# A graph network in one kernel: at most two scatters on their way, and four sets of blocks in place of three

## The chip, the cores and the metric

The kernel runs on one core of one Trainium2 chip. The metric is the device time of one execution in microseconds (us): 5878.37 us before the change, the median of 3 runs (5878.09 to 5882.56). Engine names are those of the profile: PE (matmul) and PEld (its weight load), DVE (vector), ACT (scalar), POOL (GpSimd), SP (the engine that issues most DMAs).

## The reference, cut to what matters

A graph has 6250 nodes with 128 features and 106,250 edges, sorted by destination. Four residual blocks follow each other, each on `h = relu(layernorm(x))`:

```
deg[i]  = number (or summed weight) of the edges into i;  dinv = rsqrt(deg)
gcn(h, W, b): (segment_sum of (h@W)[src] * dinv[src]*dinv[dst] over dst) + b
x += L0: gcn whose edge weights are sigmoid(gelu([h_src,h_dst]@w1+b1)@w2+b2)
x += L1: relu(gcn(relu(gcn(h, W1, b1)), W2, b2))
x += L2: m = relu(h@Wm1+bm1)@Wm2+bm2; agg = segment_sum(m[src]); MLP of [h, agg]
x += L3: gcn(relu(gcn(relu(gcn(h)))))
```

After L0 there are six sums over the same edges. They all use the same matrix of edge counts, and so the kernel builds this matrix once.

## The kernel before, in words

Nodes stand in 49 blocks of 128 (`DB = 49`). The work has these stages, each in program order on its engine.

**Preparation** (about 90 us): lists of sources and destinations, layernorm of the nodes, a table in DRAM.

**First pass over the edges** (220 groups of 4 tiles of 128 edges). POOL gathers rows of the table with indirect DMAs (`gather`, L655), PE and ACT and DVE make the edge weights, and PE sums the degrees. Beside it DVE and ACT find repeated edges inside runs of 1024 edges (`compare`, `dedupe`), which leaves for each edge a count (`count16`) and an address in the count matrix `adj` (`place`). SP stores rows for the second pass, and zeroes `adj`, one block per four groups.

**Scatters.** When POOL has issued its last gather it runs `scatter(g)` for g = 0 to 207 (L663 to L669): four indirect DMAs each, one per column `s`, 832 in all. Each writes 128 counts of two bytes to `adj` in DRAM. Before scatter k POOL waits until scatter k-4 has landed (`after(pool, scattered[s], 16 * g)`, L667, one semaphore per column), and for `s = 0` also for `deduped`. The waits stand in POOL's own stream, and nothing but scatters is behind them.

**Second pass over the edges** (220 groups again). PE spreads dinv of the sources (L963), DVE picks (`pick`, L1399), ACT weighs one-hot matrices (`weigh`, L771), PE sums rows (`sum_rows`, L972), DVE adds them (L1413). Then the L0 result is finished (`conv`), all in about 110 us.

**Dense stage.** The six sums are q = 0 to 5. For each block of destinations w, PE multiplies the 49 chunks of `adj` (as `halves` in SBUF, loaded by SP, five buffers of up to 25 chunks, `AR = 5`) with the node features, kept as three bf16 parts: one matmul of 128x128 by 384 columns per chunk (L1030). The list `UNITS` (L71 to L79) sets the order for all engines:

- *whole*: all 49 chunks of block w of sum q, then one matmul that adds the rows of `spare` (L1040), then DVE reduces the three parts (`reduce_sum`, L1499) and makes the next layer's input.
- *spare*: edges that cross runs have their counts in an extra block. There is one extra block for each set of destination blocks (`SETS`), because a set may begin before the scatters of the next set have landed. A spare unit of q = 0 takes 49 matmuls, a split on DVE, and a sum of the counts into `spare_sum` (`combine`, L1520), which q > 0 uses.
- *early*: part of the chunks of a block of sum q = 1, done between the sets of q = 0. DVE reduces them and adds them to `acc` (`take_early`, L1532 to L1536). The *late* unit of q = 1 does the rest.

In q = 1 (the message layer) each block is normalized before it goes on: DVE runs `take_sums` (reduce, two scalar_tensor_tensor, L1490 to L1496 with a square root on ACT between), PE turns the result (`turn_source`, L1053) after two thirds of the *next* unit's chunks, then multiplies (`up`, L1064); `down` (L1073) follows after the first third of the unit after. After its own `take_sums` DVE does `set_table` of the block before (L1571, L1503 to L1506). PE's order is written out in the loop at L1085 to L1106, which cuts each unit's chunks in three parts (`cuts`).

Before it loads the spare block of a set, SP reads from `needed` how many scatters must have landed and waits for them (L583 to L591).

Of the kernel before, what the change touches and what calls it, by code (L numbers as in the profile page):

```python
# [44 lines left out]

DB = -(-N // P)

SETS = ((0, 26), (26, 41), (41, 49))
EARLIER = len(SETS) - 1
SPARE = DB  # L50
BLOCKS = DB + len(SETS)
ROW_BITS, SRC_BITS = 13, 6
# [14 lines left out]

EARLY = [[(0, 24, 0, 25)], [], []]  # L70
UNITS = []  # L71
for n, (w0, w1) in enumerate(SETS):
    UNITS += [(0, SPARE + n, 0, DB, "spare")] + [(0, w, 0, DB, "whole") for w in range(w0, w1)]
    UNITS += [(1, w, c0, c1, "early") for b0, b1, c0, c1 in EARLY[n] for w in range(b0, b1)]

LATE_C = {w: max((c1 for one in EARLY for b0, b1, c0, c1 in one if b0 <= w < b1), default=0) for w in range(DB)}
for q in range(1, LAYERS):
# [15 lines left out]
def after(eng, sem, value):  # L93

    if value > 0:
        eng.wait_ge(sem, value)
# [10 lines left out]
def build(nc, a, out):  # L107
# [13 lines left out]
    with ExitStack() as ctx, ExitStack() as early:  # L121
# [3 lines left out]
        def sem(name):  # L125
            return ctx.enter_context(nc.semaphore(name))
# [273 lines left out]
        scattered = [sem(f"scattered{s}") for s in range(S)]  # L400
# [210 lines left out]
        def _(pool):  # L611
# [51 lines left out]
            def scatter(g):  # L663
                pool.wait_ge(deduped, g // RUN_TILES + 1)
                for s in range(S):
                    k = g * S + s
                    after(pool, scattered[s], 16 * g)  # L667
                    nc.gpsimd.indirect_dma_start(out=adj[:, :], out_offset=bass.IndirectOffsetOnAxis(ap=place[:, k:k + 1], axis=0),  # L668
                                                 in_=count16[:, k:k + 1], in_offset=None).then_inc(scattered[s], 16)  # L669

# [5 lines left out]
            for g in range(SCATTERS):  # L676
                scatter(g)
# [173 lines left out]
        def _(pe):  # L851
# [154 lines left out]
            def add_sources(u, c0, c1):  # L1006
                q, w, u0, u1, kind = UNITS[u]
                for c in range(c0, c1):
                    if c == u0:
                        after(pe, reduced, u - 2)  # L1010
                    if q > 0 and kind == "spare":
                        if c == 0:
                            pe.wait_ge(combined, 2 * len(SETS))
                        if c == DB - 2:
# [96 lines left out]
        def _(dve):  # L1111
            made = [0]

            def link(instruction):

                made[0] += 1
                instruction.then_inc(prep, 1)
                dve.wait_ge(prep, made[0])
# [19 lines left out]
            for n in range(EARLIER):  # L1138
                last = nc.vector.tensor_scalar(in_sets[:, n, :], last_window[:, :], float(SETS[n][1]), None, ALU.is_lt)
            link(last)  # L1140
# [101 lines left out]
            nc.vector.tensor_tensor(in_runs, of_runs, ps_carry_b.unsqueeze(2).to_broadcast([P, SLOTS, RUN_TILES]), ALU.is_equal)  # L1242
            link(nc.vector.tensor_scalar(late[:, :], ps_carry_b, float(P * SETS[0][1]), None, ALU.is_ge))
            for n in range(1, EARLIER):
# [376 lines left out]
```

## Time and profile before

| | us |
|---|---|
| median of 3 runs | 5878.37 |
| profiled execution, its time | 5869.91 |
| its span on the core | 5868.2 |
| PE busy / DVE busy / ACT busy / POOL busy | 3758.9 / 2498.4 / 1229.7 / 1736.7 |
| matmul L1030, 14553 of them | 2476.2 busy |
| scatters L668, 832 of them | 869.1 busy, 270.5 idle ahead of them |

The span is cut into 40 slices of 146.7 us. The page shows PE busy to 3 or 4 tenths in slices 1 to 10, near 0 in slices 11 to 18, and to 9 tenths from slice 22 to the end; POOL is busy to 7 tenths in slices 8 to 17 and then stops. Since matmuls overlap, two figures are kept apart: the mean length of one (326 ns) and the distance from one to the next.

### The profile page before, as it was taken

The page shows a single profiled execution, that of the slowest core. Times are in us where ns is not written, and L with a number is a line of the kernel's source. Part 1 is how long each engine was busy: PE and PEld are TensorE (multiplying, and loading weights), DVE is VectorE, ACT ScalarE, POOL GpSimd, SP SyncE. Part 2 cuts the span into 40 slices and gives each one's busy share as a digit, 9 for nine tenths or more (in the row PEclk, how much of TensorE's full clock was granted, in tenths as well). Part 3 has the DMA queues.
Part 4 walks back from the last instruction along what each step waited for, and adds up shares of the span by engine and source line. Part 5 has one row for each costly group of instructions (what it writes and reads, how often), then busy time and mean ns, then how long its engine had stood idle before and what let it go on. Part 6 is the DMA issues. An engine that isn't in the chain of part 4 may idle for free.

```text
span 5868.2 us, 82106 instructions
## 1 busy us (share of the span) xinstructions
PE 3758.9 (64%) x26427; PEld 2570.5 (44%) x26427; DVE 2498.4 (43%) x11277; ACT 1229.7 (21%) x3130; POOL 1736.7 (30%) x1749
## 2 busy tenths in 40 slices
PE   3444444444000000007667999999999999999999
PEld 2333333333000000006555666666666666666666
DVE  6666766676101000009997222454344333333111
ACT  2454444444000000005554000111111000000000
POOL 4665666666777777760000000000000000000000
PEclk7555555555555555559998999999999999999999
DMA  5777777776100000007772565455555566566665
GB/s 151 233 228 232 230 232 224 232 231 207 22 1 23 11 7 11 11 8 231 238 236 98 177 193 181 160 164 176 160 165 167 170 191 192 181 190 191 187 199 170
DMA packets 456936, 925.35 MB, mean 158 GB/s; under 512 B 81052, under 2 KB 318060, under 8 KB 449868
## 3 DMA queue, kind: packets, MB, share of 16 engines
q1 hardware_dynamic: 382668, 830.57, 44.1%
q0 software_dynamic: 69312, 87.75, 6.2%
q8 instruction: 230, 3.77, 0.3%
q10 hardware_dynamic: 4544, 1.77, 0.1%
q14 instruction: 182, 1.49, 0.1%
HBM read 739.99 MB, written 179.87 MB: 157 GB/s over the span
## 4 chain that ended last, share of the span: by engine, by line
PE 46%; another core or an unknown queue 24%; DVE 16%; issue 8%; ACT 3%; DVEq 1%; DMA 0%; SPq 0%; ACTq 0%
PE ps L1030 40%; DVE same L1296 3%; DVE inv_all L1399 3%; PE ps L1064 1%; ACT apart L746 1%; DVE onehot_b L1327 1%; DVEq L478 1%; PE ps L1073 1%; DVE scaled L1339 1%; DVE acc L1413 1%; DVE h L1413 1%; ACT apart L749 1%; PE ps L1040 1%; DVE pre L1335 1%
## 5 line engine op out<-in xcount | busy, mean ns | idle before, releaser
L1030 PE MATMUL ps<-parts,halves 128*128 128x384 bf16 x14553 | 2476.2, 326 | 6.1 <-DVE parts L1470 5.6
L1030 PEld LDWEIGHTS ps<-parts,halves 128*128 128x128 f16 x14553 | 1425.4, 98 | 887.8 <-DVE parts L1470 7.1
L660 POOL DMA_INDIRECT rows<-table,src_of x880 | 842.7, 958 | 583.9 <-DVE pre L1335 299.9
L668 POOL DMA_INDIRECT adj<-count,place x832 | 869.1, 1045 | 270.5 <-issue 270.5
L1499 DVE TENSOR_REDUCE summed_f<-ps 128x128 f32<-128x384 f32 x277 | 154.5, 558 | 1394.8 <-PE ps L1040 1307.7
L940 PE MATMUL ps<-dst_mlp,onehot_t 128*128 x2640 | 364.5, 232 | 562.0 <-issue 329.5
L963 PE MATMUL ps<-inv_parts,low_t 128*128 128x49 bf16 x2640 | 130.7, 189 | 673.3 <-issue 523.9
L940 PEld LDWEIGHTS ps<-dst_mlp,onehot_t 128*128 128x128 bf16 x2640 | 275.8, 104 | 640.7 <-issue 583.9
L1399 DVE SCALAR_TENSOR_TENSOR inv_all<-chunk_iota,chunk_of,ps 128x49 f32<-128x49 f32 x880 | 181.9, 263 | 798.9 <-remote 796.8
L771 ACT ACTIVATE onehot<-plain,norm 128x128 f32<-128x128 bf16 x880 | 281.0, 390 | 1016.5 <-issue 754.3
L1296 DVE SCALAR_TENSOR_TENSOR same<-spare_sum,key,ps 128x128 bf16<-128x128 f32 (+2 forms) x832 | 488.1, 588 | 6.5 <-DMA spare_sum<-key_list 6.3
L972 PE MATMUL ps<-rows,onehot 128*128 128x128 f32 x1760 | 286.0, 298 | 267.2 <-issue 264.8
L954 PE MATMUL ps<-weight_parts,onehot_b 128*128 128x4 bf16 x880 | 132.5, 185 | 483.1 <-DVE weight_parts L1362 243.3
L963 PEld LDWEIGHTS ps<-inv_parts,low_t 128*128 128x128 bf16 x2640 | 94.2, 98 | 726.5 <-issue 540.1
L825 ACT COPY source_t<-ps 128x128 f32<-128x128 f32 x196 | 52.2, 266 | 1610.1 <-PE ps L1053 1610.1
L972 PEld LDWEIGHTS ps<-rows,onehot 128*128 128x128 f32 x1760 | 241.3, 205 | 276.0 <-issue 273.1
L954 PEld LDWEIGHTS ps<-weight_parts,onehot_b 128*128 128x128 bf16 x880 | 92.0, 105 | 562.6 <-issue 540.3
L720 ACT COPY onehot_t<-ps 128x512 bf16<-128x512 bf16 x220 | 128.2, 583 | 907.6 <-remote 732.1
L1335 DVE TENSOR_TENSOR pre<-ps,rows 128x256 f32<-128x256 f32 x220 | 91.8, 417 | 284.9 <-remote 284.9
L746 ACT ACTIVATE apart<-spare_sum,key 128x768 bf16<-128x768 f32 x208 | 204.2, 982 | 13.8 <-DMA spare_sum<-key_list 4.8
L749 ACT ACTIVATE apart<-apart,ones 128x768 bf16<-128x768 bf16 x208 | 205.6, 988 | 6.8
L1327 DVE TENSOR_SCALAR onehot_b<-window_iota_b,local_dst 128x128 bf16<-128x128 bf16 x880 | 162.8, 259 | 0.0
(255 smaller groups left out, 3586.7 us busy)
## 6 DMA issues: line engine op xcount, KB each, us to landing
halves<-adj SPq DMA_DIRECT2D x297, 800.0 KB, 4.5
halves<-adj SPq DMA_DIRECT2D x297, 768.0 KB, 4.4
adj<-slot_of SPq DMA_DIRECT2D x52, 1568.0 KB
h_rows<-rows SPq DMA_DIRECT2D x220, 256.0 KB
rows<-h_rows SPq DMA_DIRECT2D x220, 256.0 KB
spare_sum<-key_list SPq DMA_DIRECT2D x104, 512.0 KB
onehot_list<-onehot_b SPq DMA_DIRECT2D x220, 128.0 KB
low_row<-low_list SPq DMA_DIRECT2D x220, 128.0 KB
```

The source lines that it names most:

```text
L660: nc.gpsimd.indirect_dma_start(out=rows_0[:, g % RING, s, :], out_offset=None, in_=table[:, :], in_offset=bass.IndirectOffsetOnAxis(ap=src ...
L668: nc.gpsimd.indirect_dma_start(out=adj[:, :], out_offset=bass.IndirectOffsetOnAxis(ap=place[:, k:k + 1], axis=0), in_=count16[:, k:k + 1], ...
L746: nc.scalar.activation(apart[:, 0:r, :], key_row[:, n % KEYS, 0:r, :], ACT.Abs, bias=key[:, t:t + 1], scale=-1.0).then_inc(distant, 1)
L749: nc.scalar.activation(apart[:, 0:r, :], apart[:, 0:r, :], ACT.Relu, bias=ones[:, 0:1], scale=-1.0, accum_out=cross[:, batch % 2, r * S + ...
L771: last = nc.scalar.activation(onehot[:, g % SUMS, s, :], plain[:, g % KEPT, s, :], ACT.Copy, scale=norm[:, g % NORMS, s:s + 1])
L940: last = nc.tensor.matmul(ps_mlp[:, g % 2, s, :], onehot_t[:, g % 2, s, :], dst_mlp[:, bass.ds(window[s], 1), part, :].rearrange("p o m -> ...
L954: last = nc.tensor.matmul(ps_deg[:, bass.ds(window[s] * (PARTS + 1), PARTS + 1)], onehot_b[:, g % HELD, s, :], weight_parts[:, g % 2, s, : ...
L963: last = nc.tensor.matmul(ps_inv[:, g % 2, s, :], low_t[:, g % 2, s, :], inv_parts[:, part, :], start=part == 0, stop=part == PARTS - 1)
L972: last = nc.tensor.matmul(products[:, g % SUMS, s, :], onehot[:, g % SUMS, s, :], rows[:, g % RING, s, :], start=True, stop=True)
L1030: last = nc.tensor.matmul(ps_sum[u % 3], halves[:, n % AR, c - at, :], parts[q % 2][:, c, :, :].rearrange("p t d -> p (t d)"), start=(c == ...
L1296: nc.vector.scalar_tensor_tensor(same[r % 2][:, 0:r + 1 - r0, :], key_row[:, n % KEYS, r0:r + 1, :], key[:, t:t + 1], ps_weight[:, CROSS - ...
L1399: last = nc.vector.scalar_tensor_tensor(inv_all[:, s, :], chunk_iota[:, 0, :], chunk_of[:, k:k + 1], ps_inv[:, j, s, :], ALU.is_equal, ALU ...
```

## The change

Two things. POOL waits, ahead of scatter k, also for scatter k-2 to have landed (`s - 2` is -2 or -1 for the first two columns, which names columns 2 and 3 of the group before). And `SETS` has four sets in place of three, with other early units: 26 blocks of 25 chunks after the first set, 10 of 25 and 36 of 10 after the second, 9 of 35 (in two loads) after the third.

```
-SETS = ((0, 26), (26, 41), (41, 49))
+SETS = ((0, 26), (26, 36), (36, 45), (45, 49))
-EARLY = [[(0, 24, 0, 25)], [], []]
+EARLY = [[(0, 26, 0, 25)], [(26, 36, 0, 25), (0, 36, 25, 35)], [(36, 45, 0, 35)], []]
 (in scatter(g), for each s:)
                     after(pool, scattered[s], 16 * g)
+                    after(pool, scattered[s - 2], 16 * (g + 1 if s >= 2 else g))
                     nc.gpsimd.indirect_dma_start(out=adj[:, :], ...)
```

An entry of `EARLY` is (first block, end of blocks, first chunk, end of chunks). `LATE_C` (L76) takes from it where the late unit of a block begins: chunk 25 for blocks 0 to 23 before; chunk 35 for blocks 0 to 44 after. `BLOCKS`, the number of blocks of `adj` that are zeroed, goes from 52 to 53, and `EARLIER` from 2 to 3.

## Rows read from the trace of the kernel before

**Rows 1.** Busy time by stage: us, PE, PEld, DVE, ACT, POOL, PEclk, DMA share, GB/s.
```profile
1475.00:1811.00 336.00, 15.14 (x109) 11.01 (x109) 33.78 (x123) 16.07 (x32) 256.51 (x254) 0.50 0.05 9
1811.00:2615.00 804.00, 72.80 (x322) 49.27 (x322) 30.45 (x200) 19.16 (x60) 612.55 (x579) 0.50 0.05 11
2615.00:3085.00 470.00, 298.48 (x3962) 261.38 (x3962) 427.82 (x2782) 253.03 (x793) 0.00 (x0) 0.95 0.72 222
...
3196.00:5868.00 2672.00, 2665.62 (x17018) 1721.44 (x17016) 887.16 (x2937) 205.68 (x735) 0.00 (x0) 1.00 0.57 179
```

**Rows 2.** Waits between 1475 and 2615 us: total, times, longest.
```profile
ACT onehot L771 <- issue: 754.3, 15, 54.7
DVE inv_all L1399 <- remote: 732.5, 15, 54.7
```

**Rows 3.** Groups of POOL: all scatters.
```profile
L668 POOL DMA_INDIRECT adj<-count,place x832 | 869.1, 1045 | 270.5 <-issue 270.5
```

**Rows 4.** Timeline within the scatters: start, length, instruction, idle before.
```profile
2131.04 0.98 POOL L668 DMA_INDIRECT adj<-count,place  x1 [0.30 <-issue]
2132.32 0.97 POOL L668 DMA_INDIRECT adj<-count,place  x1 [0.31 <-issue]
```

**Rows 5.** Timeline of PE and PEld a little later.
```profile
2142.66 0.10 PEld L963 LDWEIGHTS ps<-inv_parts,low_t 128*128 128x128 bf16 x1 [2.69 <-issue]
2144.06 0.20 PE L963 MATMUL ps<-inv_parts,low_t 128*128 128x49 bf16 x1 [2.60 <-issue]
```

**Rows 6.** The last scatter, in the timeline of POOL.
```profile
2613.34 1.09 POOL L668 DMA_INDIRECT adj<-count,place  x1 [0.30 <-issue]
```

**Rows 7.** DMA busy tenths from 2613 to 2617 us, 0.1 us per digit.
```profile
DMA  0000001100000000000011000000000000000000
```

**Rows 8.** The first gather of the first pass, in the timeline.
```profile
90.11 1.25 POOL L660 DMA_INDIRECT rows<-table,src_of  x1 [41.84 <-DMA table<-acc]
```

**Rows 9.** DMA busy tenths from 87 to 91 us, 0.1 us per digit.
```profile
DMA  9988998300000000028300000000000000000000
```

**Rows 10.** Another restart of POOL, in the timeline.
```profile
30.66 1.16 POOL L652 DMA_INDIRECT acc<-src_list,tile_of  x1 [18.36 <-DMA dst_list<-lists]
```

**Rows 11.** GB/s of the DMAs from 27 to 31 us, 0.1 us per figure.
```profile
GB/s 323 333 312 225 215 220 195 189 190 149 133 128 128 128 118 108 102 92 77 67 61 51 26 20 5 0 0 0 0 0 0 0 0 0 0 0 0 0 0 0
```

**Rows 12.** A gather released by a compute engine, in the timeline.
```profile
1451.12 0.42 DVE L1335 TENSOR_TENSOR pre<-ps,rows 128x256 f32<-128x256 f32 x1
...
1451.81 0.95 POOL L660 DMA_INDIRECT rows<-table,src_of  x1 [3.22 <-DVE pre L1335]
```

**Rows 13.** Two early units of 25 chunks, in the timeline of DVE.
```profile
3440.57 0.56 DVE L1499 TENSOR_REDUCE summed_f<-ps 128x128 f32<-128x384 f32 x1 [3.12 <-PE ps L1030]
...
3444.63 0.56 DVE L1499 TENSOR_REDUCE summed_f<-ps 128x128 f32<-128x384 f32 x1 [3.12 <-PE ps L1030]
```

**Rows 14.** One late unit of 24 chunks, in the timeline of all engines.
```profile
3842.47 0.56 DVE L1499 TENSOR_REDUCE summed_f<-ps 128x128 f32<-128x384 f32 x1 [1.02 <-PE ps L1040]
...
3845.41 0.14 PEld L1053 LDWEIGHTS ps<-ident,source 128*128 128x128 f32 x1 [0.32 <-issue]
3845.44 0.30 PE L1053 MATMUL ps<-ident,source 128*128 128x128 f32 x1
...
3846.38 0.29 DVE L1506 TENSOR_TENSOR parts<-left_d,parts 128x128 bf16<-128x128 f32 x1
...
3846.88 0.61 PE L1064 MATMUL ps<-source_t,w_L_gnn_Wm 128*128 128x128 f32 x4
...
3847.69 0.56 DVE L1499 TENSOR_REDUCE summed_f<-ps 128x128 f32<-128x384 f32 x1 [1.01 <-PE ps L1040]
```

**Rows 15.** Two whole units of q = 1, in the timeline of DVE.
```profile
3893.29 0.56 DVE L1499 TENSOR_REDUCE summed_f<-ps 128x128 f32<-128x384 f32 x1 [4.45 <-PE ps L1040]
3902.41 0.56 DVE L1499 TENSOR_REDUCE summed_f<-ps 128x128 f32<-128x384 f32 x1 [4.45 <-PE ps L1040]
```

**Rows 16.** The third spare unit of q = 0, in the timeline of PE.
```profile
3678.37 8.13 PE L1030 MATMUL ps<-parts,halves 128*128 128x384 bf16 x49
```

## The prediction

> **What bounds the kernel now.** I read first the busy time by stage [rows 1]. It shows three regimes. From 3196 us to the end PE is busy for 2665.6 of 2672 us: the dense stage is bound by PE alone, at full clock. From 2615 to 3085 us the second pass over the edges runs, bound by DVE (428 of 470 us). From 1475 to 2615 us POOL does the scatters, and nothing else makes headway: PE 88 us, DVE 64 us of 1140. Then the waits of that stretch [rows 2]: fifteen waits of up to 54.7 us on ACT and on DVE, 754 and 733 us in total; those on DVE are put down to something outside the engines. Fifteen groups of the second pass get done there, at 56 us each (the longest wait and one round of work), where later each takes 470/205 = 2.3 us. The timeline shows how: PE brings an instruction to its start every 1.4 us, a weight load at 2142.66 and its matmul at 2144.06 [rows 5], while POOL starts a scatter every 1.28 us and idles 0.30 us between two [rows 4]. A group of the second pass needs 40 PE instructions (20 matmuls, 20 loads), and 40 x 1.4 = 56 us. It ends when the scatters do. So the path is: first pass, all 832 scatters, second pass, dense stage. Every us on the scatters is a us on the kernel, and so is every us for which PE waits in the dense stage; the DMAs are not full in either (0.05 and 0.57).
>
> One thing follows at once. The dense stage begins at 3196 us, 580 us after the last scatter [rows 6]. Sets exist so that the dense stage may begin before all scatters have landed; no such wait is there to be shortened, and the new sets and early sums can only cost.
>
> **Part 1, the second wait.** It adds no transfer. First, does it hold anything back? The last scatter starts at 2613.34 [rows 6], and its packets move from 2615.0 to 2615.2 [rows 7]: 1.86 us from its start to the end of its data. The scatter before it started 1.40 us earlier, and its packets lie at 2613.6 to 2613.8, as far behind its own start. At 1.28 us a scatter [rows 4], scatter k-2 began 2.56 us before k does and has had its data written 0.7 us before. So two at a time is what is on the way already. The wait costs only what it takes POOL to go on from it. Today the wait is for k-4, whose data ended 3.2 us ahead, and POOL's stream can have instructions ready while it works; with the new wait the next scatter can't be made ready before k-2 has landed, which is when k-1 is nearly done.
>
> What a restart takes, from both sides. Low: a gather released by DVE starts at 1451.81, when DVE ended at 1451.54 [rows 12]: 0.27 us. Then k could start 1.86 + 0.27 = 2.13 us after k-2 (some tenths more for the semaphore of a DMA), less than 2.56, and the wait is free. High: two restarts from a landing. The data that the first gather waited for ended at 89.0 [rows 9], and it started at 90.11 [rows 8]: 1.11 us. In the other, the data ended at 29.5 [rows 11] and the indirect DMA started at 30.66 [rows 10]: 1.16 us. With 1.16, two scatters take 1.86 + 1.16 = 3.02 us, 1.51 each. Now one takes (869.1 + 270.5)/832 = 1.37 us [rows 3], so the high end is 832 x 0.14 = +117 us; a few scatters that DVE's work holds back add some, and I keep +130. By the row of 1.11 it is 2.97/2 = 1.485 and 832 x 0.115 = +96. A gain from the wait alone would need PE to be let go; that is the first rival. This is the same kind of instruction waiting for a DMA, so I go by these rows and not by that of 0.27; but both were first of their kind after a long rest, and ran 1.25 and 1.16 us in place of 0.95, so I take off a fifth. **+75 us**. Behind POOL's wait stand only more scatters; who waits for them is PE, which is slow until they end. In 75 us more of this, 75/56 = 1.3 groups more get done, worth 2.3 us each: **-3 us**.
>
> The Trainium skill, "DMA: Bandwidth & Descriptors", section "Anatomy of one DMA — SWDGE (gpsimd) path", gives about 2.0 us of fixed cost to one DMA from POOL, most of it the receipt of the write, and 0.05 us to the dispatch. By these figures the new wait is met 0.5 us ahead of need and costs nothing: an estimate of +0 in place of +75. The first figure agrees with the 1.86 us of [rows 6, 7]; the second is far under the 1.1 us that [rows 8, 9] leave between data and start, of which it may be only a part.
>
> **Part 2, the fourth set.** One more spare unit of q = 0: 49 matmuls at 8.13/50 = 0.1625 us [rows 16] = **+8 us** on PE. Its split and the sum of the spare counts go on DVE beside the next unit's 49 matmuls, as they do now. One more block to be zeroed lies in the first pass, before the last gathers; DMAs are 0.72 busy there, and POOL does not wait for it. A fourth wait of SP for scatters is met 580 us before.
>
> **Part 3, early and late units.** The chunks are the same in number, so PE's matmuls are. Early: 26 x 25 + 10 x 25 + 36 x 10 + 9 x 35 = 1575 chunks against 600; late: 45 blocks of 14 chunks against 24 of 24. Early units follow each other on PE without a gap: 4.06 us for 25 chunks [rows 13], 0.1625 each. One of 10 chunks takes 1.63 us; DVE needs 0.56 + 0.35 us and two hops, about 1.0, so it still keeps up; SP loads 320 KB for each, with four loads ahead (6.5 us), where 800 KB land in 4.5 us on the page. So early units cost 0, and +10 if a load of small pieces falls behind (for the range).
>
> Late units are another matter. A whole unit of q = 1 takes 9.12 us [rows 15], so one of 24 chunks should take 9.12 - 25 x 0.1625 = 5.06; it takes 3847.69 - 3842.47 = 5.22 [rows 14]. The rest is PE waiting 0.3 us for DVE's chain (`take_sums`), which must be through before PE may turn the block: the turn starts 2.97 us behind the reduction. From there to the next reduction it is 2.25 us, of which 8 chunks are 1.30. With 14 chunks only 4 are left behind the turn: the period is 2.97 + 2.25 - 4 x 0.1625 = 4.57 us. Since the turn now waits for DVE's chain and the other 10 chunks are long done, nothing shortens it. DVE's own work per unit ends 3846.67 - 3842.47 = 4.20 us behind its start, less than 4.57, so it isn't the bound. PE alone would need 9.12 - 35 x 0.1625 = 3.43. It waits 1.14 us in each of 45 late units, 51 us, and no longer 0.16 in 24, 4 us: **+47 us**. Bounds: +35 if the two chains overlap better, +60 if PE's second step (L1064), which needs ACT's copy of the turned block, comes 0.2 late as well.
>
> **Sum.** 5869.9 + 75 - 3 + 8 + 47 = 5997 us for an execution like the profiled one. The runs' median lies 8 us above that execution; I forecast **6004 us** for the median. Less than 0.2% (12 us) can't be told from no change.
>
> **Rivals.**
> 1. *PE is let go: faster.* The pace of PE hangs on POOL's unbroken work: 1.4 us an instruction in the scatters, none of this after them. If gaps of 0.4 to 0.5 us between scatters in place of 0.30 let PE through, the second pass moves under the scatters. Wholly: the end of the first pass no longer takes 336 us [rows 1], the second pass (220 x 2.3 = 506) is over at about 2000 us, the dense stage starts at 2115 and ends at 2115 + 2672 + 55 = 4842, plus the waits of sets for scatters: about 4860. In part: at twice the pace the tail halves and the remaining 1047 us hold 37 groups, 22 more, 50 us: 5954, still slower. It decides from 127/2.3 = 55 groups more on, a pace of under 0.4 us. For it: the sets would then be of use, and the starving is tied to POOL. Against it: even gaps of 0.3 us at 1.4 us spacing free nothing now, one scatter is still always on its way, and two are already the most that are.
> 2. *The wait is free* (restart of 0.27 us): 6004 - 72 = 5932. This is also the case in which the wait does not do what it says, since no third scatter was ever on its way.
> 3. *The restart is dearer*, past 1.3 us, or two semaphores per instruction slow POOL: 1.6 us a scatter, +190: 6120.
> 4. *The late units don't wait*, because the trace's 0.3 us is no true bound: 6004 - 47 = 5957.
>
> **Chances.** My forecast 0.48 (its own range 5970 to 6055), rival 2 0.20, rival 4 0.07, rival 3 0.07, rival 1 0.14 of which three quarters end faster than before, 0.04 for things I don't see, spread over both sides. Faster by over 0.2%: 0.13; within 0.2%: 0.03; slower 0.84. Range 5910 to 6080: it holds the forecast, rivals 2 and 4 and the bounds of the late units, and leaves out most of rivals 1 and 3.
>
> **What the profile after would show.** Part 1: POOL idle per scatter 0.4 to 0.5 us in place of 0.3, scatters from 1475 to about 2690, and 56 us a group in the second pass as before. Part 2: four spare units of q = 0. Part 3: reductions 4.57 us apart in late units, 0.7 us or more of idle ahead of each turn, no idle of PE in early units. I am wrong if PE's instructions come closer than 1.4 us while POOL scatters, if scatters keep 1.37 us, or if late units take 3.4 us.

## The result, and the profile after

The changed kernel takes 5241.04 us, the median of 4 runs (5238.31 to 5247.42), against 5878.23 us for the kernel before in the same series. The ratio is 0.8918, with a 95% interval of 0.8907 to 0.8929: 637 us faster, where 126 us slower was forecast. The profiled execution took 5239.61 us with a span of 5237.9 us.

The page of the kernel after, busy tenths in 40 slices of 131 us:

```profile
PE   3444444444446666008987779899999999999999
POOL 3565665656653335664454541000000000000000
```

PE is no longer dark while POOL scatters: the second pass (slices 13 to 16) and the dense stage run beside scatters that go on as far as slice 25. Only two slices of PE are dark, 17 and 18. The groups of the scatters and of the dense matmuls, busy time and mean, and idle ahead of them with its releaser:

```profile
L670 POOL DMA_INDIRECT adj<-count,place x832 | 820.1, 986 | 874.1 <-DMA adj<-count,place 610.9 <-issue 263.2
L1032 PE MATMUL ps<-parts,halves 128*128 128x384 bf16 x14602 | 2490.0, 327 | 387.9 <-DMA halves<-adj 387.9
```

POOL now idles 874.1 us ahead of scatters in place of 270.5 [rows 3], and PE waits 387.9 us for `adj`, where the forecast had no such wait. Busy time by stage (columns as in [rows 1]):

```profile
1485.00:1521.00 36.00, 14.71 (x107) 10.70 (x106) 25.32 (x119) 16.38 (x34) 21.66 (x23) 0.50 0.20 59
1530.00:2030.00 500.00, 340.73 (x4376) 300.82 (x4376) 475.12 (x3070) 280.94 (x880) 193.25 (x199) 0.94 0.77 230
...
2115.00:2374.00 259.00, 0.00 (x0) 0.00 (x0) 8.76 (x51) 0.00 (x0) 169.07 (x175) 0.50 0.03 5
```

The end of the first pass, 109 matmuls that took 336 us [rows 1], is over 36 us after the first scatter (two of them fall a little later). The whole second pass then takes 500 us, 2.3 us a group, where fifteen groups took 56 us each [rows 2]. Meanwhile POOL starts 199 scatters in 500 us, one in 2.5 us, not in 1.37. So PE has nothing to do from 2102 to 2374: the dense stage waits for the scatters of its first set, and again ahead of the second and third set. These three waits are 384.2 of the 387.9 us. In the timeline of PE:

```profile
2374.17 4.14 PE L1032 MATMUL ps<-parts,halves 128*128 128x384 bf16 x15 [272.58 <-DMA halves<-adj]
...
2779.07 3.36 PE L1032 MATMUL ps<-parts,halves 128*128 128x384 bf16 x10 [52.42 <-DMA halves<-adj]
...
3038.94 6.33 PE L1032 MATMUL ps<-parts,halves 128*128 128x384 bf16 x26 [59.23 <-DMA halves<-adj]
```

**Where the time went.** In the kernel before the first scatter started at 1475 and the first dense matmul here:

```profile
3173.57 6.66 PE L1030 MATMUL ps<-parts,halves 128*128 128x384 bf16 x40
```

From first scatter (1475 and 1486) to first dense matmul it was 1698 us and is now 888: -810. The gathers end 11 us later (+11). From there to the last matmul of the dense loop it was 2688 us (3173.6 to 5861.9) and is now 2857 (2374.2 to 5231.5): +169, of which the waits of the later sets are 112, one more spare unit 8, and early and late units together 47: 45 late units at 4.56 us for what was 24 at 5.21 and 21 at 9.12, and 975 more chunks of 0.1625 us in early units. The sum is -630, which is what the two profiled executions differ by.

Two timelines of POOL show the scatters beside the second pass, and at its end, when nothing else moves data:

```profile
1645.75 0.97 POOL L670 DMA_INDIRECT adj<-count,place  x1 [2.53 <-DMA adj<-count,place]
1647.02 0.97 POOL L670 DMA_INDIRECT adj<-count,place  x1 [0.30 <-issue]
1650.87 0.97 POOL L670 DMA_INDIRECT adj<-count,place  x1 [2.88 <-DMA adj<-count,place]
...
2102.84 0.96 POOL L670 DMA_INDIRECT adj<-count,place  x1 [0.30 <-issue]
2104.44 0.97 POOL L670 DMA_INDIRECT adj<-count,place  x1 [0.64 <-issue]
2105.72 0.97 POOL L670 DMA_INDIRECT adj<-count,place  x1 [0.30 <-issue]
```

In quiet the gaps are 0.30 and 0.64 in turn, 2.88 us for two scatters, 1.44 each. Beside the second pass (DMA share 0.77) many gaps are 2.5 to 2.9 us: scatters land late among the loads of `rows` and `plain`, and POOL now stands until they have. By the semaphore events of the trace a scatter lands 2.13 us behind its start in quiet (2115 to 2374 us, median) and 4.0 us behind it beside the second pass (1530 to 2030 us).

### The profile page after: what moved, and what is told of

It reads as the page before. It is cut to its first block, busy times and chain, and to the rows that moved or that the text cites. A ratio compares the mean times of both kernels' runs of the same rounds, so it can differ in the third digit from the quotient of the medians.

```text
span 5237.9 us, 83120 instructions
## 1 busy us (share of the span) xinstructions
PE 3742.2 (71%) x26476; PEld 2553.8 (49%) x26476; DVE 2559.0 (49%) x11400; ACT 1230.5 (23%) x3130; POOL 1685.5 (32%) x1749
## 4 chain that ended last, share of the span: by engine, by line
PE 37%; POOL 20%; issue 20%; DMA 19%; DVE 3%; SPq 0%; POOLq 0%; ACT 0%; another core or an unknown queue 0%; DVEq 0%
PE ps L1032 32%; DMA adj<-count,place 19%; POOL rows L660 15%; POOL adj L670 5%; PE ps L1066 1%; PE ps L1042 1%; PE ps L1018 1%; PE ps L1078 1%; PE ps L1055 1%; PE ps L1075 1%; DVE summed_f L1501 0%; DVE norm_d L1553 0%; DVE source L1498 0%; DVE stats_d L1492 0%; DVE x L1554 0%
## 5 line engine op out<-in xcount | busy, mean ns | idle before, releaser
L1032 PE MATMUL ps<-parts,halves 128*128 128x384 bf16 x14602 | 2490.0, 327 | 387.9 <-DMA halves<-adj 387.9
L670 POOL DMA_INDIRECT adj<-count,place x832 | 820.1, 986 | 874.1 <-DMA adj<-count,place 610.9
L1501 DVE TENSOR_REDUCE summed_f<-ps 128x128 f32<-128x384 f32 x335 | 186.9, 558 | 1785.2 <-PE ps L1042 1195.2
L974 PE MATMUL ps<-rows,onehot 128*128 128x128 f32 x1760 | 269.0, 299 | 4.4 <-ACT onehot L773 4.4
L974 PEld LDWEIGHTS ps<-rows,onehot 128*128 128x128 f32 x1760 | 230.7, 205 | 5.0 <-ACT onehot L773 5.0
L965 PE MATMUL ps<-inv_parts,low_t 128*128 128x49 bf16 x2640 | 110.4, 189 | 165.5 <-DVE low_t L1393 103.0
L1345 DVE TENSOR_REDUCE logit<-scaled 128x4 f32<-128x256 f32 x220 | 92.4, 420 | 113.7 <-remote 69.0
```

Of the source, the lines that this page charges most:

```text
L965: last = nc.tensor.matmul(ps_inv[:, g % 2, s, :], low_t[:, g % 2, s, :], inv_parts[:, part, :], start=part == 0, stop=part == PARTS - 1)
L974: last = nc.tensor.matmul(products[:, g % SUMS, s, :], onehot[:, g % SUMS, s, :], rows[:, g % RING, s, :], start=True, stop=True)
L1032: last = nc.tensor.matmul(ps_sum[u % 3], halves[:, n % AR, c - at, :], parts[q % 2][:, c, :, :].rearrange("p t d -> p (t d)"), start=(c == ...
L1501: nc.vector.tensor_reduce(into, ps_sum[u % 3].rearrange("p (t d) -> p d t", t=PARTS), AX.X, ALU.add).then_inc(reduced, 1)
```

## The experiments

**A second level of the kernel before.** Each set of kernels below ran as one job on one chip, the kernel before among them. That kernel has two levels, and one job shows only one of them:

| job, chip | kernel before, us | kernels, us (ratio, 95% interval) |
|---|---|---|
| the result above | 5878.2 | after 5241.0 (0.892) |
| 1, chip 10 | 4555.7 | e1 5043.1 (1.107, 1.105 to 1.109); e2 4582.4 (1.006, 1.004 to 1.008); e3 4580.0 (1.005, 1.004 to 1.007); e4 4901.9 (1.076, 1.074 to 1.078) |
| 2, chip 8 | 5913.8 | e5 5912.8; e6 5280.9 (0.893, 0.891 to 0.894) |
| 3, chip 12 | 4557.1 | e7 5039.6 (1.107); e8 4581.9 (1.005); e9 4898.5 (1.076); e10 4664.6 (1.024, 1.022 to 1.026) |
| 4, chip 2 | 4555.9 | e11 4669.5 (1.024); e12 4583.3 (1.006) |
| 5, 6, 7, chips 15, 3, 1 | 4554.0, 4560.3, 4560.3 | e13 4924.0; e14 4936.6; e15 4938.4 |
| 8, chip 6 | 5879.9 | e16 5282.7 |
| 9, chip 3 | 5907.0 | e17 5900.3 |
| 10, chip 9 | 5875.0 | e18 5235.7 (0.891, 0.889 to 0.894) |

Call the level of 4556 us open and that of 5875 to 5914 us starved. Chip 3 was open in job 6 and starved in job 9, so the level does not belong to a chip. The kernels e5 and e13 to e17 ran once each.

**e1, e2: the wait alone, the sets alone.** e1 is the kernel before with the new wait; e2 is the changed kernel without it.

```
 e1   SETS, EARLY as before
+                    after(pool, scattered[s - 2], 16 * (g + 1 if s >= 2 else g))
 e2   SETS, EARLY as after
-                    after(pool, scattered[s - 2], 16 * (g + 1 if s >= 2 else g))
```

> The kernel before with the second wait alone; its three sets and 24 early units stay. Theory A (the wait lets PE go, the sets only make use of it): the second pass is over near 2110 us, as with the whole change; PE then waits for the scatters of blocks 0 to 25, as far as about 2380; after 27 units and 24 early ones (2380 + 220 + 98 = 2700) the next set needs 41/49 of the scatters, 700 of 832, near 2860 to 2900, 16 units take it to about 3010, the last set waits to about 3150 (the last scatter landed), and what is left of the dense stage is 2672 - 350 - 98 = 2224 us: 5300 to 5400 us. Rival B (the new sets and their early units are what lets PE go, or both are needed): PE is starved as before, and the time is 5878 plus the price of the wait, 5930 to 5960.

> The change without the second wait: four sets and the deeper early sums alone. Theory A: PE is starved as before, 56 us per group of the second pass until the last scatter near 2615; the time is that of before plus one spare unit (+8) and the late units (+47): 5878 + 55 = 5933, within 10. Rival B (the sets let PE go): 5240 or less.

Neither figure was met, since the job was open: the kernel before took 4556. The second pass of e2 there, by stage and in the timelines of POOL and PE:

```profile
1231.00:1725.00 494.00, 326.02 (x4361) 285.86 (x4362) 472.93 (x3052) 279.89 (x877) 348.37 (x360) 0.98 0.83 232
```
```profile
1399.13 0.96 POOL L668 DMA_INDIRECT adj<-count,place  x1 [0.30 <-issue]
1399.77 0.94 PE L972 MATMUL ps<-rows,onehot 128*128 128x128 f32 x7
1400.40 0.97 POOL L668 DMA_INDIRECT adj<-count,place  x1 [0.30 <-issue]
1401.52 0.48 PE L963 MATMUL ps<-inv_parts,low_t 128*128 128x49 bf16 x12 [0.80 <-DVE low_t L1391]
```

POOL starts scatters at 1.27 us with gaps of 0.30, as in [rows 4], and PE does 12 matmuls in 0.48 us beside them. So the cadence of POOL does not starve PE by itself; it does so in some jobs. In this job, where PE is free without it, the wait only costs. Beside the second pass e1 starts 193 scatters in 493 us, e2 360 in 494; PE waits three times for `adj`, 551.8 us in sum, and the kernel takes 487 us more. The sets and early sums cost 27 us there, half of the 55 put; the kernel before has no profile in an open job, so what they give back there is not known.

**e3, e8, e12: the second wait present but always met.** **e4, e9: one wait, for k-2. e10, e11: one wait, for k-3.**

```
 e3   after(pool, scattered[s], 16 * g)
      after(pool, scattered[s - 2], 16 * (g if s >= 2 else g - 1))
 e4   after(pool, scattered[s - 2], 16 * (g + 1 if s >= 2 else g))      and no other
 e10  after(pool, scattered[s - 3], 16 * (g + 1 if s >= 3 else g))      and no other
```

> The changed kernel with its second wait moved back by four scatters: scatter k waits for k-4 and for k-6. The instruction for the second wait is still in POOL's stream, but it never holds POOL back. Theory A (what counts is that POOL is held back): PE is starved as before, 1.28 to 1.4 us a scatter, 5933 as with the sets alone. Rival C (a further semaphore instruction in POOL's stream is what lets PE through): 5240 or less.

> The changed kernel with the wait for k-2 alone; the wait for k-4 is dropped (k-2 had itself waited for k-4). No more than two scatters are on their way, as in the change, but there is one wait per scatter as in the kernel before. In the changed kernel a held scatter starts 0.74 us behind the landing of k-2; in the kernel before one wait went with its scatter. Theory A1 (PE is let go wherever no third scatter is given to the queue): about the time of the change, somewhat faster where a held scatter restarts sooner: 5100 to 5240. Theory A2 (PE is let go only by the gaps in which POOL stands and waits, 0.64 us in place of 0.30 for every second scatter): a scatter lands 2.0 us behind its start, k starts 2.56 behind k-2, so in quiet the wait is always met, POOL makes no new gap and PE is starved: 5933.

These ran in the open job 1, so neither theory was tried. What they price there: a second wait that never holds POOL costs nothing (4580.0 against 4582.4 of e2). One wait for k-2 costs 320 us (4901.9 against 4582.4). In quiet it makes only one gap in four wide, that of the scatter which also waits for `deduped` (the other three have one wait, and k-2 has landed when they are ready):

```profile
1902.43 0.97 POOL L668 DMA_INDIRECT adj<-count,place  x1 [0.30 <-issue]
1904.04 0.97 POOL L668 DMA_INDIRECT adj<-count,place  x1 [0.64 <-issue]
```

**e5, e6: both kernels once more.** Unchanged kernels, for a profile of each in one job.

> The kernel before, unchanged, for a profile of its own on whatever chip this run gets. On the chip of the first four experiments its runs took 4556 us where the first chip took 5878. Theory K (the chips differ in whether PE is starved beside POOL's scatters): either 5870 to 5885 with 56 us per group of the second pass under the scatters, or 4550 to 4565 with 2.3 us per group there; nothing between. Theory R (it changes from run to run on one chip): a time that does not agree with the other runs of this kernel in the same series.

> The changed kernel, unchanged. Theory K: where PE is starved in the kernel before, 5241 again (ratio 0.89). Where it isn't, the second wait only holds the scatters back: 2.25 to 2.5 us each beside other work in place of 1.37. There the wait alone took 5043 with PE idle 155 and 96 us ahead of the second and third set; the four sets and deeper early sums cover 251 - (53 + 60) = 140 us of it and cost 8 + 47: 5043 - 140 + 55 = 4960, within 40 (ratio 1.09).

The job was starved, and both came out as in the result (0.8925). In e5 PE has 426 matmuls in the 1140 us of the scatters. The first 556 us of the scatters in e6:

```profile
1521.00:2077.00 556.00, 351.54 (x4509) 307.72 (x4509) 509.28 (x3205) 297.09 (x912) 226.32 (x228) 0.91 0.71 212
```

Of theory K one half holds (two levels, nothing between), the other, that it is a matter of the chip, fell with job 9.

**e7 to e12** were meant for a starved job and got open ones.

> The kernel before with the second wait alone, as in the first experiment, for a chip on which PE is starved in the kernel before (5878 to 5914). If it runs there. Theory A (the wait lets PE go, the sets only make use of it): the first gather phase ends 310 us later than on the chip of the first experiment (1514 against 1202), the rest is as there: 5043 + 310 = 5350, within 40. Theory B (the sets are needed too): 5930 to 5960. If it runs where PE isn't starved: 5043 again.

> The changed kernel with its second wait moved back to k-6, where it never holds. On a chip with PE starved: Theory A (POOL must be held back): 5933 to 5970, PE starved as before. Theory C (the further semaphore instruction lets PE through): under 5000, since nothing then slows the scatters. Where PE isn't starved: 4580 again.

> One wait per scatter, for k-2. On the chip of the first experiments its gaps in quiet were 0.30 us for three scatters of four and 0.64 for the fourth. On a chip with PE starved: Theory A1 (two on their way at most is what counts): PE goes; 4902 + 310 = 5210. Theory A2 (the gaps count, and each second one must be wide): PE gets perhaps one chance in four scatters, the second pass takes long, 5500 to 5950. Where PE isn't starved: 4902 again.

> The changed kernel with one wait per scatter, for k-3: three on their way at most. In quiet k-3 has landed 1.8 us ahead of need, so nothing is held; beside other work a landing takes 3.5 to 4 us, so that three allow one scatter each 1.2 to 1.45 us. On a chip with PE starved: Theory A1 or A2: in quiet nothing holds POOL, so once starved PE stays starved: 5933 to 5970. If it is let go none the less: dense stage from about 2180 and 2727 us more, 4960. Where PE isn't starved: the scatters take 1.4 to 1.5 us, 4585 to 4650.

> One wait per scatter, for k-3. Two chips so far took 4556 for the kernel before and let PE go beside the scatters, two took 5878 to 5914 and starved it; this is for one that starves it. Theory A1 or A2 (PE is let go where POOL is held back): in quiet k-3 has landed 1.8 us ahead of need, nothing holds POOL, PE stays starved: 5933 to 5970. Rival (three on their way are few enough): dense stage from about 2200 and 2727 us more, 4960 to 5000. Where PE isn't starved: 4665 again.

e7, e8, e9 repeated e1, e3, e4 within 0.1%, and e12 repeated e3 once more. e10 and e11 are new: three on their way cost 1.024 with the sets, against 1.006 with four, a pace of 1.67 us beside the second pass (296 scatters in 493 us) and 1.58 over all 832. In the open level holding POOL back has a price that grows with each scatter fewer: 1.006, 1.024, 1.076.

**e13 to e16: seven ways in one kernel.** Since the level of a job can't be chosen, one kernel was made that goes through all ways in turn.

```
 kind = "ABFCDEG"[g // 8 % 7]          # 32 scatters each; sets as before
 A  after(scattered[s], 16 * g)                       k-4, as before
 B  A, and after(scattered[s - 2], ...)               k-4 and k-6, always met
 F  A, behind nc.gpsimd.memset(scrap, 0.0)            wider gaps, nothing held
 C  k-3    D  k-2    E  k-4 and k-2, as the change    G  k-1
```

> The kernel before (three sets), whose scatters change their waits every 32 scatters, in turn: A wait for k-4 (as before); B for k-4 and k-6 (two waits, never held); F as A, with a memset of 128x256 on POOL ahead of each scatter (wider gaps, nothing held); C for k-3; D for k-2 alone; E for k-4 and k-2 (as in the change); G for k-1 (one on its way). On a chip that starves PE I read PE's instructions per us in each stretch of the second pass. Theory A1 (at most two on their way): PE runs in D, E and G, starved (0.7 a us) in A, B, F, C. Theory A2 (the gaps count, whatever makes them): PE runs in E and G and in F, little in D, starved in A, B, C. Theory B (the sets): starved in all seven, since the sets are those of before. Theory C (the further semaphore instruction): PE runs in B and E. By A1 or A2 the second pass ends after about seven free stretches, near 2200 us. On a chip that doesn't starve PE: free in all, 4750 to 4850, and the stretches give only the pace of the scatters.

> The seven ways a fourth time, for a chip that starves PE (kernel before at 5878 to 5914). Theory A1 (at most two on their way): PE runs in D, E and G, 0.7 instructions a us in A, B, F, C. Theory A2 (the gaps count): PE runs in E, G and F, little in D, 0.7 a us in A, B, C. Theory B (the sets): 0.7 in all seven. Theory C (the semaphore instruction): PE runs in B and E. On a chip that doesn't: 4924 to 4938 again, PE free in all seven.

e13, e14 and e15 (e14 and e15 with the wider memset of e16) got open jobs: 11 to 18 PE instructions a us in every stretch of the second pass, whatever the way. e16 got a starved one. Its stretches A B F C D E of the first turn and A B F C of the second (the instructions of PE and of PEld are the first two counts in brackets):

```profile
1484.00:1525.00 41.00, 3.30 (x24) 2.43 (x24) 5.58 (x24) 1.08 (x3) 31.25 (x33) 0.50 0.08 13
1525.00:1566.00 41.00, 1.11 (x9) 0.88 (x9) 2.10 (x14) 1.84 (x4) 31.38 (x34) 0.50 0.05 10
1566.00:1623.00 57.00, 10.75 (x77) 7.70 (x77) 21.01 (x86) 13.02 (x26) 47.66 (x63) 0.50 0.05 10
1623.00:1685.00 62.00, 39.75 (x460) 36.46 (x461) 53.10 (x309) 28.03 (x88) 37.33 (x33) 0.78 0.75 216
1685.00:1764.00 79.00, 51.10 (x703) 44.51 (x703) 76.00 (x491) 44.71 (x140) 31.39 (x33) 1.00 0.80 236
1764.00:1846.00 82.00, 55.40 (x725) 48.93 (x724) 78.33 (x509) 46.66 (x147) 30.63 (x32) 0.96 0.78 234
...
1991.00:2032.00 41.00, 8.64 (x61) 6.02 (x60) 5.89 (x36) 3.83 (x12) 31.12 (x33) 0.60 0.18 53
2032.00:2073.00 41.00, 3.38 (x14) 2.45 (x15) 2.26 (x14) 1.28 (x4) 31.39 (x34) 0.50 0.02 0
2073.00:2129.00 56.00, 18.27 (x152) 15.43 (x151) 16.96 (x109) 9.19 (x29) 48.27 (x64) 0.56 0.25 68
2129.00:2179.00 50.00, 31.90 (x332) 28.23 (x330) 35.65 (x229) 21.47 (x68) 30.72 (x32) 0.77 0.67 178
```

Read the counts. In B, where the further semaphore instruction is there and holds nothing, PE brings 18 and then 29 instructions in 41 us; the second, 0.7 a us, is the starved pace of [rows 5]: theory C falls. The sets are those of before, and PE runs in C, D, E and G: theory B, that the sets let it go, falls. In F the wait is that for k-4, as before, but the memset puts 0.70 us or more between two scatters: PE gains, 2.7 and 5.4 a us on the mean, and is free in the last part of each F (from about 1600 and from 2110). PE, free at the end of G, falls back within 10 us of A's start at 1991. So no wait for k-2 is needed: setting POOL's scatters apart lets PE go. Whether it is the space that does it, or the other work of POOL in that space, no run tells. C was a surprise: three on their way suffice, at least for a PE that C finds free.

The third A of e16, at the start of the dense stage, shows the same under the wait for k-4 alone. While the loads of `adj` make landings late and POOL stands 1.2 to 2.7 us at a time, PE does its matmuls one behind the other. The last such break is the first of the rows below; from about 2426 us, 11 us later, PE stands, once for 38.48 us:

```profile
2414.98 0.97 POOL L686 DMA_INDIRECT adj<-count,place  x1 [2.69 <-DMA adj<-count,place]
...
2475.51 1.19 PE L1091 MATMUL ps<-w_L_gnn_W,hidden 128*128 128x128 f32 x4 [38.48 <-issue]
```

**e17: C, D and E, each behind a starved stretch.**

```
 kind = "ACADAE"[g // 8 % 6]
```

> The kernel before (three sets); every 32 scatters the waits change, in the order A C A D A E: A wait for k-4, C for k-3, D for k-2 alone, E for k-4 and k-2. So C, D and E each begin after 41 us of A. On a chip that starves PE, by PE's instructions per us: Theory A2 (gaps count): in quiet C has gaps of 0.30 us as A has, so PE stays starved (under 1 a us) in C that follows a starved A; D has one gap of 0.64 in four and frees it late or not; E frees it within 40 us. Theory A3 (three on their way are few enough): PE runs in C as well, within 10 us of its start. On a chip that doesn't starve PE, free in all, about 4750, and only the paces: A 1.27 to 1.5, C 1.3 to 1.9, D 1.4 to 2.4, E 1.5 to 2.6 us.

The job was starved. Stretches C, D and E from 2064 us on (those of A between them left out), and one scatter within E:

```profile
2064.00:2107.00 43.00, 4.59 (x16) 3.14 (x16) 0.00 (x0) 0.00 (x0) 32.34 (x32) 0.50 0.06 13
...
2152.00:2199.00 47.00, 3.98 (x17) 2.19 (x16) 2.17 (x14) 1.28 (x4) 34.05 (x33) 0.50 0.06 11
...
2243.00:2293.00 50.00, 4.53 (x18) 3.05 (x18) 2.17 (x14) 1.28 (x4) 31.14 (x32) 0.50 0.05 11
...
2260.01 0.97 POOL L686 DMA_INDIRECT adj<-count,place  x1 [3.30 <-issue]
```

Starved in all of them, the change's own wait E included (36 instructions in 50 us), and 5900 us for the kernel. A starved PE brings no loads (DMA share 0.05), scatters land soon, and a wait for k-2 then makes gaps of up to 0.67 us, 0.30 in turn. Two gaps in this E are wider, 1.70 and 3.30 us, and PE stays starved behind them: one such break alone does not let it go. Theory A2 is right for C and D and wrong for E within 50 us.

**e18: the change, its first 32 scatters under the old wait.** Is PE in the changed kernel never caught, or does it get free?

```
+                    if g >= 8:
                         after(pool, scattered[s - 2], 16 * (g + 1 if s >= 2 else g))
```

> The changed kernel, but the second wait begins with scatter 32, 41 us after the first. Theory H (the state keeps itself: a going PE brings loads, loads make landings late, late landings hold POOL, and a held POOL lets PE go; a starved PE leaves the queues quiet, scatters land in 2.1 us, the gaps are 0.30 and 0.64 in turn and PE stays starved), in a job that starves PE: starved to the last scatter at 1.46 us each, 56 us a group, as my prediction had it: 1480 + 32 x 1.28 + 800 x 1.46 = 2690 for the last scatter, and about 6000 us in all (5960 to 6040). Theory A (the second wait frees PE wherever it stands, it needs some 50 us): 5241 and 40 more, 5260 to 5350. In a job that doesn't starve PE: 4930 to 4960.

Theory H, my reading of e17, falls for a starved stretch at the end of the first pass: 5235.7 us in a starved job, as fast as the change. A wait that begins only when the second pass is under way and starved, as in e17, was not tried for longer than 50 us. The stretch of the old wait, the rest of the first pass under the new one, and the second pass:

```profile
1482.00:1521.00 39.00, 0.59 (x4) 0.42 (x4) 3.53 (x14) 0.00 (x0) 29.76 (x31) 0.50 0.08 14
1521.00:1618.00 97.00, 14.50 (x105) 10.55 (x105) 25.37 (x114) 16.06 (x32) 62.07 (x64) 0.50 0.05 10
1626.00:2121.00 495.00, 335.42 (x4373) 296.08 (x4374) 472.46 (x3066) 280.97 (x880) 189.15 (x196) 0.96 0.78 232
```

Under the new wait the last 105 of 109 matmuls of the first pass take 97 us, where the old wait took 336 us for them [rows 1] and the mix of e17 346 us. Then, between 1618 and 1626, comes the step to the free state, and it has a mark. When the second pass begins and its first loads are issued, one scatter takes 6 to 7 us. That scatter in the kernel before, in the changed kernel with what follows, and in e18, and behind each timeline the busy time of 20 us after it (e17, which has this scatter in a stretch A, is like the kernel before: 6.78 us, then 17 scatters and no instruction of PE in 20 us):

```profile
1805.42 6.27 POOL L668 DMA_INDIRECT adj<-count,place  x1 [0.89 <-issue]
```
```profile
1813.00:1833.00 20.00, 0.00 (x0) 0.00 (x0) 0.00 (x0) 0.00 (x0) 15.15 (x16) 0.50 0.19 45
```
```profile
1521.72 6.92 POOL L670 DMA_INDIRECT adj<-count,place  x1 [0.30 <-issue]
...
1532.59 0.97 POOL L670 DMA_INDIRECT adj<-count,place  x1 [2.68 <-DMA adj<-count,place]
```
```profile
1530.00:1550.00 20.00, 15.82 (x180) 14.43 (x180) 17.58 (x119) 12.16 (x39) 7.09 (x8) 0.81 0.82 254
```
```profile
1618.61 6.38 POOL L670 DMA_INDIRECT adj<-count,place  x1 [0.31 <-issue]
```
```profile
1626.00:1646.00 20.00, 14.02 (x180) 12.68 (x180) 17.36 (x121) 11.60 (x37) 6.61 (x8) 0.89 0.85 248
```

Under the wait for k-4 POOL goes straight on, 16 scatters in the next 20 us, and PE brings nothing. Under the new wait the loads make landings late, POOL stands 2.68 us, 8 scatters start, and PE brings 360 instructions in 20 us. From there the state can keep itself: PE at work brings loads (share 0.82), loads bring late landings, and these bring one break of 2.5 us and more after another.

But that break is not what parts the two. They have parted within the long scatter, while POOL starts nothing: SP, which issues the loads, takes 0.70 to 1.40 us for each of them there in the kernel before, e5 and e17, and 0.32 to 0.43 for every one in the change, e6, e16 and e18 (rows in the last section). So what lets PE go lies ahead of the long scatter or at its start. In the change, e6 and e18 the scatters ahead of it start under the new wait, with gaps of 0.30 and 0.64 and a wider one now and then (1.91 and 1.53 us in the change and e18); in e16 they are those of F; in the three that stay starved the gaps are 0.30, but for one or two of 0.69 to 0.89 us just ahead of it in the kernel before and e5. Which part of this does it is not shown.

## Why the prediction was wrong, point by point

- **The step that failed** is the sentence of part 1 that PE "is slow until they end", with its term of 1.3 groups, -3 us, and "56 us a group in the second pass as before". All 220 groups went at 2.3 us; the term measured -810 us (first scatter to first dense matmul, all of part 1 in it) where +72 was put. In the changed kernel the end of the first pass took 36 us and the second pass 500 us, beside scatters that went on for 1150 us more. The argument for it, "even gaps of 0.3 us at 1.4 us spacing free nothing now, one scatter is still always on its way, and two are already the most that are", took the number on their way as the cause and the 1.86 us from start to end of data as a constant. It holds only while the queues are quiet; once loads flow, landings come 4.0 us behind the start in place of 2.13, and the wait holds POOL for 2.5 us and more at a time (610.9 us in sum). e16 shows that the count allowed is not what matters: F has four scatters allowed and still lets PE go. How the gaps of 0.64 get PE out before loads flow stays open: e18 and e6 do it, E of e17 does not in 50 us.
- **Rival 1** named what happened: its mechanism (gaps let PE through) and, within 15 us, when PE would be through with the second pass: 2115 us, against 2102. Its chance was put at 0.14. Its time, 4860, was too low by 380 us, because it left the scatters at 1.37 us each: they took 2.04 on the mean, and PE's waits for `adj` are 387.9 us. 4842 + 388 = 5230, against a span of 5238.
- **The price of the wait in quiet** was right. From 2115 to 2374 us there are 175 scatters in 259 us, 1.48 each; from 1811 to 2615 in the kernel before there were 579 in 804 us, 1.39 each. That is 0.09 us more, and 832 x 0.09 = 75. The two steps that make it up are a landing 2.13 us behind the start and, by the events of the trace, 0.74 us from the landing to the start of the scatter that waited. From the end of the data, which is what the prediction counted from, it is 2.88 - 1.86 = 1.02 us, a little under the rows of 1.11 and 1.16. The row of 0.27 belongs to an instruction with a single wait: in e4 a scatter that waits for k-2 alone starts 0.27 us behind its landing (median, beside the second pass), and in quiet that wait is free, as rival 2 had it. The Trainium skill's page "DMA: Bandwidth & Descriptors" (section "Anatomy of one DMA — SWDGE (gpsimd) path") gives about 2.0 us of fixed cost and 0.05 us to the dispatch. By these the wait of the change would have been free, an estimate. The first figure agrees with the 2.13 us measured in quiet; beside the second pass it is 4.0, and in place of the second stand the 0.74 us and a gap of 0.64 before every second scatter.
- **The fourth set** cost what was put (+8 us, one more unit of 49 matmuls). But "no such wait is there to be shortened" and "the new sets and early sums can only cost" held only for the starved kernel. With PE free the sets count: the dense stage starts at 2374 with 381 of the 832 scatters still to come. That start hangs on the first set, which is blocks 0 to 25 in both kernels. What the new sets and early sums shorten are the waits ahead of the later sets: 250 us in e1, which has the wait and three sets (551.8 less its first wait of 301.8), and 115 us after (387.9 less 272.6). Less the 55 us that they cost, this is some 80 us gained, an estimate, since the two ran at different levels.
- **The late units** were right to 0.01 us: the period is 4.56 us (4.57 put), and the turn begins 2.97 us behind the reduction, at 3311.46, as put. From the timeline of DVE and PE after:

```profile
3308.49 0.56 DVE L1501 TENSOR_REDUCE summed_f<-ps 128x128 f32<-128x384 f32 x1 [0.36 <-PE ps L1042]
...
3311.46 0.30 PE L1055 MATMUL ps<-ident,source 128*128 128x128 f32 x1 [0.86 <-DVE source L1498]
...
3313.05 0.56 DVE L1501 TENSOR_REDUCE summed_f<-ps 128x128 f32<-128x384 f32 x1 [0.36 <-PE ps L1042]
```

- **Early units** cost nothing, as put.

What the profile before could have told: that PE is not slow wherever POOL issues indirect DMAs. In the gather phase POOL did make breaks, one of 3.22 us in [rows 12], with the same kind of DMA, and PE was busy to 3 or 4 tenths there. I held that against "one scatter is always on its way" too lightly. That a job could also let PE run beside an unbroken run of scatters, no row of it could tell.

**What stays open.** What decides the level of a job. Whether the wait alone, without the sets, does it all in a starved job (e1 and e7 got open jobs only; e16, one run, shows just that the sets are not needed to free PE), and what three on their way take there. How the wider gaps let PE go, and why e17 did not see it. And what the whole change takes in an open job; it was not run there. e1 (1.107, wait without sets) and e4 (1.076, sets with one wait) are its nearest relations, and both are slower than before. No kernel tried is best at both levels: 4556 us is the kernel before in an open job, 5236 to 5241 the change and e18 in a starved one.

## What to carry to other kernels

An engine that brings one instruction in 1.4 us, beside an engine that issues DMAs without a break, may be in a state and not at a pace: ask what would break the issuer's run before you price anything at that pace, and measure the kernel in several jobs. A wait that looks free at the landing times of a quiet queue is not the same wait when the work that it lets go fills the queue. And a rival that turns the sign needs its knock-on effects priced as carefully as the forecast.

## What the runs showed of the hardware

The same kernel on the same chip took 4560 us in one job and 5907 in another. Already the gather phase differs: PE did 3603 matmuls between 200 and 1100 us in e2 and 2861 in the kernel before, by these rows of e2 and of before:

```profile
200.00:1100.00 900.00, 496.20 (x3603) 362.06 (x3602) 782.03 (x3836) 562.22 (x1100) 682.46 (x715) 0.50 0.90 287
```
```profile
200.00:1100.00 900.00, 393.32 (x2861) 288.91 (x2861) 623.68 (x3041) 438.68 (x883) 545.98 (x573) 0.50 0.73 231
```

It is not PE alone that starves. Within the long scatter at the start of the second pass SP, which issues its loads, takes 0.70 or 1.40 us for each in the kernel before, and 0.43 after the change:

```profile
1807.32 1.40 SPq L575 DMA_DIRECT2D rows<-h_rows  x1
1809.42 0.70 SPq L577 DMA_DIRECT2D plain<-onehot_list  x1
```
```profile
1522.93 0.43 SPq L575 DMA_DIRECT2D rows<-h_rows  x1
1523.40 0.43 SPq L577 DMA_DIRECT2D plain<-onehot_list  x1
```

PE's 1.40 us [rows 5] is twice the same 0.70. So PE and SP may be held by one and the same thing; no run here shows what it is.
